# An attention and feed-forward kernel on one core: the first maxima ahead of later batches' work, and two weight loads moved out of the first scatters

## What is computed

```python
q = (layernorm(x) @ Wq); k, v = split(ctx @ Wkv)
q, k = rope(q, pos), rope(k, pos)                       # 32 heads of 8
w = softmax(einsum('bqhd,bkhd->bhqk', q, k) / sqrt(8))
x = x + einsum('bhqk,bkhd->bqhd', w, v).reshape(b, n, 256) @ Wout + bout
h = layernorm(x)
s = top_k(h @ gate_w, 2).sum(-1)
y = square(relu(h @ up_w)) @ down_w + (h @ expert_weight) * s
x = x + layernorm(y) * gamma + beta
```

## Time and profile before

| | |
|---|---|
| median of 3 runs | 213.78 us (211.82 to 215.93) |
| the profiled execution's own time | 210.77 us |
| its span, first to last instruction | 209.0 us |
| mean granted TensorE clock in it | 0.978 |
| PE busy | 190.0 us, 91% |
| DVE busy | 142.8 us, 68% |
| ACT busy | 120.5 us, 58% |
| POOL busy | 84.5 us, 40% |

### The profile page before, as it was taken

One profiled execution on the slowest core, in us unless ns is written; L12 is line 12 of the kernel. 1 busy time (PEld: TensorE's weight loads), 2 busy tenths in 40 slices (PEclk: granted clock), 3 DMA queues, 4 the chain that ended last, 5 costly groups with the idle time before them and its releaser, 6 DMA issues.

```text
span 209.0 us, 6609 instructions
## 1 busy us (share of the span) xinstructions
PE 190.0 (91%) x2506; PEld 161.0 (77%) x2506; DVE 142.8 (68%) x297; ACT 120.5 (58%) x275; POOL 84.5 (40%) x169
## 2 busy tenths in 40 slices
...
PEclk9999958999999999999999999999999999999997
...
DMA packets 15999, 13.15 MB, mean 63 GB/s; under 512 B 2912, under 2 KB 15584, under 8 KB 15968
## 3 DMA queue, kind: packets, MB, share of 16 engines
...
...
HBM read 5.13 MB, written 1.05 MB: 30 GB/s over the span
## 4 chain that ended last, share of the span: by engine, by line
PE 66%; DMA 10%; SPq 6%; DVE 4%; issue 4%; POOL 3%; ACT 3%; ACTq 1%; POOLq 0%; DVEq 0%
PE ps L823 24%; PE ps L991 12%; PE ps L940 10%; PE ps L856 9%; PE ps L817 6%; PE ps L846 4%; DMA qstack<-mT 3%; SPq L377 3%; DMA x_sb<-in_x 3%; DMA qstack<-hi_q 2%; ACT probs L627 2%; DMA kstack<-lo_k 1%; SPq L437 1%; ACTq L377 1%; DVE xn L409 1%
## 5 line engine op out<-in xcount | busy, mean ns | idle before, releaser
L744 DVE TENSOR_REDUCE mneg<-ps 128x2 f32<-128x512 f32 x128 | 81.0, 683 | 15.2 <-PE ps L846 15.0
L627 ACT ACTIVATE probs<-ps 128x512 f32<-128x512 f32 x128 | 69.1, 595 | 15.3 <-PE ps L856 13.9
L856 PEld LDWEIGHTS ps<-qstack,kstack 32*128 32x128 f32 x512 | 32.7, 185 | 14.6 <-issue 10.3
L856 PE MATMUL ps<-qstack,kstack 32*128 32x128 f32 x512 | 40.0, 282 | 3.2 <-DMA qstack<-mT 1.5
L940 PE MATMUL ps<-probs,vaug 128*32 128x128 f32 x1024 | 34.0, 275 | 0.6 <-ACT probs L627 0.4
L846 PE MATMUL ps<-kstack,qstack 32*128 32x256 f32 x256 | 32.0, 338 | 2.5 <-DMA qstack<-hi_q 2.1
L823 PE MATMUL ps<-x2nT,up 128*128 128x128 f32 x256 | 31.0, 276 | 0.1
L823 PEld LDWEIGHTS ps<-x2nT,up 128*128 128x128 f32 x256 | 30.2, 192 | 0.7 <-issue 0.2
L991 PE MATMUL ps<-down,inner 128*128 128x256 f32 x128 | 29.5, 379 | 0.0
L940 PEld LDWEIGHTS ps<-probs,vaug 128*32 128x32 f32 x1024 | 26.3, 109 | 3.5 <-issue 1.6
L536 POOL TENSOR_SCALAR mnat<-mneg 128x8 fp32r<-128x8 f32 x32 | 7.6, 236 | 49.2 <-DVE mneg L744 37.8
...
## 6 DMA issues: line engine op xcount, KB each, us to landing
...
```

What stands on the lines that cost most here:

```text
L627: act.activation(probs[M % NPROBS][:, i, :, :, :], bg(("ST", M, i))[:].rearrange("p (s t n) -> p s t n", s=2, t=T), ACT.Exp, scale=SCALE). ...
L744: emptied(dve.tensor_reduce(mneg[M % NNEG][:, i, :], bg(("S", M, i))[:].rearrange("p (s k) -> p s k", s=2), AX.X, ALU.max, negate=True), ( ...
L856: return pe.matmul(bg(("ST", M, i))[:, at:at + P], kstack[b % 2][strip(i), 2 * m + s, tile(k)], qstack[b][strip(i), 2 * m + s, tile(t)], s ...
```

## The change

Only the five tables change; every instruction of before is there once, and none is new. Six things move:

- `ldup.1` leaves ACT's table ahead of the first query scatters and stands far later, behind `ldvec.2` and ahead of `aaT.0`.
- `ldvec.1` (gamma) leaves SP's table ahead of the last scatter of batch 0's keys and stands behind `sM.9`.
- On ACT `sc.q.0.0.1`, the last scatter of the first query half, goes ahead of `hi.q.0.1`.
- The maxima of rows 0 to 2: on PE `MT.0` goes ahead of `B.0.6` and `Q.1.0`, `MT.1` ahead of `xT.2.0`, and `MT.2` ahead of `Q.2.0`, `B.3.0`, `K.2` and `xT.3.0`; on POOL `mh.0` goes ahead of `nm1.2.0`, `mh.1` and `mh.2` ahead of work of batch 1 (`pad.q.1.0`) and of the zeroing of `stackq.2` and `stackq.3`; on DVE `rd.2.3` goes ahead of `dQ.q.1.0`; on ACT and SP `aMT.0` to `aMT.2` and `sM.0` to `sM.2` go ahead of batch 1's scatters beside them.
- On PE `B.2.10` now comes right behind `B.1.9`, and `Q.2.0` and `K.2` behind `B.2.10`.
- On DVE the order within a few groups of maxima changes.

A line or two of the tables:

```diff
 PE_ORDER
-... B.0.5@13 B.0.6@54 Q.1.0@0 MT.0@6
-B.0.7@12 B.0.8@76 xT.2.0@5 MT.1@4 K.2@2 B.1.9@6541 Q.2.0@0 B.2.10@5617 B.3.0@43 xT.3.0@5 MT.2@0 B.0.11@16 PV.0@0
+... B.0.5@13 MT.0@6 B.0.6@54 Q.1.0@0
+B.0.7@12 B.0.8@76 MT.1@4 xT.2.0@5 B.1.9@6541 B.2.10@5617 MT.2@0 Q.2.0@0 B.3.0@43 K.2@2 xT.3.0@5 B.0.11@16 PV.0@0
 DVE_ORDER
-rd.1.2 rd.1.0 rd.2.2 rd.1.3 rd.1.1 rd.2.0 rd.2.1 rd.3.3
-rd.3.1 rd.3.2 dQ.q.1.0 rd.4.3 rd.3.0 rd.4.2 rd.2.3 dQ.q.2.0
+rd.1.0 rd.1.2 rd.2.2 rd.1.3 rd.1.1 rd.2.1 rd.2.0 rd.3.1
+rd.3.2 rd.2.3 dQ.q.1.0 rd.3.3 rd.4.3 rd.3.0 rd.4.2 dQ.q.2.0
```

More of the change, by code:

```diff
@@ L47 @@
 ldpos ldc.0 ldx.3.0 probe ldwq stackk.0 acT.0 wpermk sin.0 sin.1 aTR.0 axT.0.0 wpermq axT.0.1 hi.k.0 sc.k.0.1
-sc.k.0.0 aV.0 acT.1 aTR.1 hi.q.0.0 ldup.1 sc.q.0.0.0 sc.q.0.0.3 sc.q.0.0.2 hi.q.0.1 sc.q.0.0.1 sc.q.0.1.0
-sc.q.0.1.3 exptab aV.1 aTR.3 axT.1.0 aTR.2 hi.k.1 acT.2 sc.k.1.1 sc.k.1.3 aMT.0 axT.2.0 aMT.1 ex.0.1 ex.0.0
-hi.q.1.0 ex.0.2 sc.q.1.0.3 ex.0.3 lddown.0 aMT.2 sc.q.1.0.5 ex.1.1 aPV.0 aMT.3 axT.3.0 ex.1.0 ex.1.2 ex.1.3
-lddown.2 ldvec.0 hi.k.2 aMT.4 ex.2.0 ex.2.1 aPV.1 hi.q.2.0 ex.2.3 ex.3.0 aMT.5 ex.3.1 ex.2.2 ex.3.2 ex.3.3
@@ new lines @@
+exptab aV.1 aTR.3 axT.1.0 aTR.2 hi.k.1 acT.2 aMT.0 sc.k.1.1 sc.k.1.3 aMT.1 axT.2.0 ex.0.1 ex.0.0 ex.0.2 aMT.2
+ex.0.3 hi.q.1.0 sc.q.1.0.3 lddown.0 sc.q.1.0.5 ex.1.1 aPV.0 aMT.3 axT.3.0 ex.1.0 ex.1.2 ex.1.3 lddown.2 ldvec.0
+hi.k.2 aMT.4 ex.2.0 ex.2.1 aPV.1 hi.q.2.0 ex.2.3 ex.3.0 aMT.5 ex.3.1 ex.2.2 ex.3.2 ex.3.3 lddown.3 aPV.2 aMT.6
+ex.4.0 ex.4.1 aPV.3 ex.4.3 ex.4.2 ex.5.1 ex.5.0 hi.q.3.0 aPV.4 aMT.7 ex.5.2 ex.5.3 ldvec.2 ldup.1 aaT.0 ex.6.0
+aMT.8 aPV.5 ex.6.1 ex.6.2 ex.6.3 ex.7.0 ex.7.1 aMT.9 aMT.10 ex.7.2 ex.7.3 aPV.6 ex.8.0 ex.8.3 ex.8.2 ex.8.1
```

46 lines of the change are left out of this document (22 added, 24 removed).

## The result

The changed kernel has a median of 221.88 us (219.81 to 225.86) against 213.53 us (211.82 to 215.93) for the kernel before in the same series. The profiled execution took 219.81 us with a span of 218.0 us, where the one of before had 210.77 and 209.0. The forecast was 212.9 us, with a range of 209.0 to 216.6. It is wrong, in sign and beyond its range.

What follows compares the result with a forecast made beforehand. PE (TensorE), busy 190.0 of 209.0 us, was taken as the bound, with time to win in its rests and low clock. 0.2 + 0.86 + 0.3 - 0.5 = 0.9 us won, giving a 212.9 us median; range 209.0 to 216.6.

Steps and rivals of the forecast that it cites:

- the start and DVE's hole: First burst 1.5 us earlier, and DVE's 1.53 us wait behind Q.1.0 taken off: 3.0 us ahead at dQ.q.2.0.
- The loads taken out of the first scatters: Start: without gamma and up load queued ahead, the query scatters land sooner; first burst 1.5 us earlier, ends 0.1 and 2.1.
- the scatters don't land sooner: Rival, first query scatters: slow for their own 64 KB in small rows, nothing won at the start; 214.4 us, chance 0.12.
- The burst behind the burst: Up to dQ.q.2.0: B.2.10 waits for its bank until 35.0 and Q.2.0 behind it; of 3.0 us, 0.2 us is left.
- The maxima on time: Scatters of row maxima: sM.2 goes out earlier, its burst's 0.86 us wait is gone; 0.3 us more for sM.4.
- The loads where they stand now: Near 60 us: the up load just ahead of sM.7 slows that scatter; 0.5 us lost, bounds nothing and 2.2 us.
- The clock falls in the new hole: Rival, PE's rest between B.1.9 and B.2.10: low clock follows, some 3.3 us lost; 216.2 us, chance 0.22.
- The holes close: Rival, first bursts: first burst at 22.13, clock stays 1.00, back-to-back bursts cost nothing; 4.8 us won, 209.0 us, chance 0.19.
- the load's worst bound: Near 60 us: the up load's largest delay, 1.7 us more, giving 217.9 us together with a clock fall behind B.1.9.

Runs made afterwards that it cites:

- the pair of one series: Kernel before and changed kernel, both with up load at 23 us and first rests filled, new order's hole filled too: 0.9774 (old order) and 1.0021 (new order).
- the 20 transposes: Changed kernel with the up load at 23 us, plus 20 idle transposes on PE between B.1.9 and B.2.10: 1.0103, against 1.0218 without them.

## Why the prediction was wrong

The ratios make a ladder from before to the changed kernel, each step one thing (the steps across series rest on ratios whose intervals partly overlap):

| from | to | what is added | step |
|---|---|---|---|
| before | 0.9846 | loads out of the first scatters, up load at 23 us | -1.5% |
| 0.9846 | 1.0103 | the new order, its hole filled | +2.6% |
| 1.0103 | 1.0218 | the hole left empty: the clock | +1.1% |
| 1.0218 | 1.0337 | the up load at 63 us | +1.2% |

The same steps in the prediction: for the first 3.0 us won (1.4%, the start and DVE's hole), for the second 3.0 - 0.2 = 2.8 us lost again in the order and 1.16 won by the maxima (0.8% lost), for the third a chance of 0.22 at 3.3 us (1.5%), for the fourth 0.5 us (0.2%). The first and the third come near; the second is three times as large, and the fourth five times. By their intervals the first two steps are clear of the noise, the third is not, and the fourth is so only in the old order.

**The loads taken out of the first scatters** (+1.5 us, ends 0.1 and 2.1). Right in mechanism, a little small. The four scatters landed in 2.5 us, and the first burst started at 22.25, 2.0 us earlier. The loads ahead of them were the cause: with the loads back (and the fourth scatter in its old place, which moves its issue by less than 0.1 us in the prediction's rows), the burst started at 24.46. With the old order and a harmless place for the load this gives 1.5% (0.9846), or 3.3 us, more than the term for the start; the clock row there also has one low slice instead of two. The rival "the scatters don't land sooner" is refuted.

**The burst behind the burst** (+0.2 us). This is the first step that failed, by its size. The hole was forecast as 32.2 to 35.0 and measured as 2.63 us, released by a DVE maximum, just as described. But B.2.10 came at 37.62 and not at 35.0, Q.2.0 ended at 43.37 and not at 38.5, and the term became -4.9 us. DVE's work was as forecast: from its first maximum at 22.75 to dQ.q.2.0 at 43.41 it has waits of 0.54, 2.54 and 5.34 us, and 12.2 us of work remain, against 12.4. Its waits were 8.4 us, where the forecast left 2.8 (38.5 - 23.3 - 12.4). Two pieces of them were missing. The DVE hole behind Q.1.0 did not close but grew from 1.53 to 2.54 us, since the clock still fell at the first bursts; and the clock fell again behind the new hole, so that Q.2.0 took 3.75 instead of 1.97 us. The 12.4 us of work that I let DVE do without a gap depended on PE being ahead of it, and ACT's exponentials hung on DVE through the scatter of `lo_q`, which the sum never asked about. Even with PE's rests filled the new order cost 2.5% in the pair of one series.

**The maxima on time** (+0.86 and +0.3). The wait of 0.86 us for sM.2's scatter is indeed gone. So is that for sM.4, which was 0.27 us at 52.73 before. The waits went as said, and nothing of it reaches the end, since PE was 3.6 us late at the burst of row 2 (50.34 against 46.70). No run has row 2's or row 4's maxima early with all else as before, so what that is worth by itself isn't shown.

**The loads where they stand now** (-0.5 us, bounds 0 and 2.2). The second step that failed. sM.7 took 5.34 us, beyond the bound of 4.65, and its burst waited 3.18 us; with the fall of the clock behind it the place costs 2.6%, 5.6 us, in the old order (1.0107 against 0.9846) and 1.2% in the new. I bounded the transfer and not the wait's consequence: this rest of PE was paid twice, as the rest and as the low clock that came after. The reason given for 0.5 us, that PE is only part of the pace there, was wrong too: in the timeline of before the burst at 61.80 already waited 0.35 us for this scatter, so it had no slack.

```profile
61.80 0.32 PE L856 MATMUL ps<-qstack,kstack 32*128 32x128 f32 x2 [0.35 <-DMA qstack<-mT]
```

The reading that I made of a rule differs from the trace here. By the packets-in-turn rule of the Trainium skill (DMA: Bandwidth & Descriptors, Queues, rings and completion order) I estimated that the load on ACT's row delays the small scatter on SP's row by little, 0.2 us in the sum; the rule itself gives no time. The runs show 4.80 and 5.34 us for 8 KB beside 512 KB on the other row, and 2.47 and 2.60 without it. The measurement decides. What holds the 8 KB back in the engines, the load's packets or the 128 KB scatters of SP's own row that the load slows too, no run shows apart.

**The rivals.** "The clock falls in the new hole", at 0.22 and 216.2 us, was the right mechanism for a part, and the 20 transposes support it: Q.2.0 back at 1.97 us, and 2.3 us in the time, though not clear of the noise. It was still too cheap, because it took the clock as the only price of the order. Rests of 2.63 and 3.18 us were both followed by the low level (0.50), as the 2.13 of before was. The Trainium skill's page TensorE: Matmul & The Clock Gate (What's actually happening) calls the low clock the default that activity lifts, and the trace agrees: with ten transposes in the first rests the profiled execution was at 1.00 throughout. Such a rule deserved more than 0.22. "The holes close" is refuted: the burst did start at 22.25, close to its 22.13, and the clock fell all the same. Short rests were left behind the first burst (0.83 us for DVE at 23.59, 0.54 us for ACT at 24.76): rests under a us, with short pieces of work between them, were followed by a fall as a long one was. The rivals had the two losses together only at the load's worst bound of 1.7 us more (217.9 us), and both were larger than that.
